# Attention tiles handled in pairs, and rotary tables loaded half a block earlier, in a transformer layer on 8 cores

## The reference

```
xn = layernorm(x)
x  = x + attn(xn) + ffn(xn)

# attn: 16 heads of 128, 4 key/value heads, causal
q, k = rope(rms_norm(xn @ Wq.T), rms_norm(xn @ Wk.T)); v = xn @ Wv.T
bias = einsum('bhsr,bhtr->bhst', Rq, Rk)        # 12 heads, rank 32, Rq = xn @ Wrq.T, Rk = xn @ Wrk.T
bias[:, :4] = (bias + bias.transpose(0,1,3,2)) * 0.5     # heads 0 to 3 are made symmetric
bias = bias * graph_scale;  heads 12 to 15 have no bias
out = softmax(mask(q k^T / sqrt(128) + bias)) v @ Wo.T

# ffn
gelu(xn @ W0.T + b0) @ W1.T + b1                # 2048 -> 8192 -> 2048
```

## Time and profile before

| | |
|---|---|
| time, median of 2 runs | 5299.11 us (5295.26 to 5302.97) |
| profiled execution | 5314.09 us |
| its span, first to last instruction of the slowest core | 5312.4 us |
| spans of all cores | 5275.7 to 5312.4 us |
| mean granted TensorE clock | 0.815 to 0.821 of full speed |
| TensorE matmuls | busy 3780.3 us, 71% |
| TensorE weight loads | busy 1343.7 us, 25% |
| ScalarE | busy 957.6 us, 18% |
| VectorE | busy 704.8 us, 13% |
| GpSimd | busy 458.6 us, 9% |
| the four query blocks | 659 to 3250 us of the span |
| feed-forward | 3260 to 5312 us of the span |

### The profile page before, as it was taken

The page is one execution under the profiler, slowest core; times in us unless marked ns, Lnnn a source line. Parts: engine busy times, 40 slices in busy tenths (PEclk is TensorE's granted clock), DMA queues, the critical chain, the costliest instruction groups (busy, mean ns, idle before and its releaser), DMA issues.

```text
span 5312.4 us, 42482 instructions; the slowest of 8 cores (5275.7 to 5312.4 us)
## 1 busy us (share of the span) xinstructions
PE 3780.3 (71%) x14112; PEld 1343.7 (25%) x14112; DVE 704.8 (13%) x1165; ACT 957.6 (18%) x1395; POOL 458.6 (9%) x548
## 2 busy tenths in 40 slices
PE   1367654446764775655775679988998899889987
PEld 0123111112111211112211123433333334333333
DVE  5522121112121111210101200000000000000000
ACT  1110022212232122232223351100110011001100
POOL 0000012211212011121011120000000000000000
PEclk9878566568576856767757789999999999999999
DMA  2201333243333433345223314445445544544454
GB/s 90 87 24 58 95 121 135 91 161 124 135 111 135 139 107 138 108 145 172 83 105 117 117 45 147 139 158 164 149 139 158 163 143 139 172 156 137 145 162 149
DMA packets 176454, 672.16 MB, mean 127 GB/s; under 512 B 22002, under 2 KB 30322, under 8 KB 152178
## 3 DMA queue, kind: packets, MB, share of 16 engines
q1 hardware_dynamic: 108146, 400.98, 23.7%
q10 hardware_dynamic: 36864, 159.40, 9.2%
q0 software_dynamic: 31232, 109.07, 5.1%
HBM read 560.32 MB, written 109.05 MB: 126 GB/s over the span
## 4 chain that ended last, share of the span: by engine, by line
PE 45%; DMA 34%; issue 5%; POOLq 5%; DVE 5%; ACT 4%; ACTq 1%; DVEq 1%; POOL 0%; SPq 0%
DMA wcbb<-wbf 18%; PE ps L723 14%; DMA wcbf<-w 9%; PE ps L750 8%; PE ps L488 5%; POOLq L131 5%; PE ps L295 3%; PE ps L619 3%; DMA wcbf<-wv 3%; PE ps L580 3%; PE ps L569 3%; DMA wbf<-wcbb 3%; PE ps L626 3%; PE ps L682 2%; ACT ar L600 1%
## 5 line engine op out<-in xcount | busy, mean ns | idle before, releaser
L750 PE MATMUL ps<-ar,wcbb 128*128 128x512 bf16 x4096 | 923.3, 382 | 155.0 <-DMA wcbb<-wbf 148.6
L723 PE MATMUL ps<-xnT,wcbb 128*128 128x512 bf16 x4096 | 914.3, 380 | 60.9 <-DMA wcbb<-wbf 44.0
L569 PE MATMUL ps<-ar 128*128 128x512 bf16 x640 | 336.4, 530 | 402.3 <-ACTq L131 400.4
L600 ACT ACTIVATE ar<-ps,cstS 128x512 bf16<-128x512 f32 x640 | 441.3, 690 | 980.1 <-DMA wcbf<-w 343.8
L750 PEld LDWEIGHTS ps<-ar,wcbb 128*128 128x128 bf16 x4096 | 388.6, 98 | 689.7 <-issue 263.7
L723 PEld LDWEIGHTS ps<-xnT,wcbb 128*128 128x128 bf16 x4096 | 386.7, 98 | 588.2 <-issue 161.2
L619 PE MATMUL ps<-ar 128*128 128x512 bf16 x640 | 332.6, 520 | 235.4 <-POOLq L131 235.2
L731 ACT ACTIVATE ar<-ps,b0S 128x512 bf16<-128x512 f32 x256 | 176.4, 689 | 1598.5 <-PE ps L723 1598.5
L488 PE MATMUL ps<-xnT,wcbb 128*128 128x512 bf16 x1024 | 273.1, 428 | 145.2 <-DMA wcbb<-wbf 85.5
L609 POOL TENSOR_TENSOR ar<-ar,maskS 128x512 bf16<-128x512 bf16 x256 | 294.5, 1150 | 795.8 <-ACTq L131 711.5
L682 PE MATMUL ps<-ar,wcbb 128*128 128x512 bf16 x1024 | 257.3, 411 | 128.6 <-DVEq L131 70.3
(11 more groups left out here) (70 smaller groups left out, 1521.4 us busy)
## 6 DMA issues: line engine op xcount, KB each, us to landing
wcbb<-wbf SPq DMA_DIRECT2D x608, 512.0 KB
wcbf<-w ACTq DMA_DIRECT2D x128, 1024.0 KB, 5.1
wbf<-wcbb POOLq DMA_DIRECT2D x160, 512.0 KB, 4.4
wcbf<-x SPq DMA_DIRECT2D x16, 1024.0 KB
wcbf<-wv SPq DMA_DIRECT2D x64, 256.0 KB
wcbf<-wq SPq DMA_DIRECT2D x16, 1024.0 KB
wcbf<-wo SPq DMA_DIRECT2D x16, 1024.0 KB
xtb<-xT ACTq DMA_DIRECT2D x64, 256.0 KB, 4.1
```

The costliest lines, as they stand in the source:

```text
L569: return e.matmul(bank[:, :], ar[:, KT_O + g * S + tt * 128: KT_O + g * S + (tt + 1) * 128], ar[:, QT_O + hh * 512:QT_O + hh * 512 + 512], ...
L600: e.activation(ar[:, PB_O + slot * 512:PB_O + (slot + 1) * 512], bank[:, :], AF.Exp, bias=cstS[:, C_NEGC:C_NEGC + 1])
L723: return e.matmul(bank[:, :], wcbb[:, slot * 2048 + ec * 128: slot * 2048 + (ec + 1) * 128], xnT[:, ec * S + sc * 512: ec * S + sc * 512 + ...
L750: return e.matmul(bank[:, :], wcbb[:, slot * 2048 + i * 128: slot * 2048 + (i + 1) * 128], ar[:, HACT_O + ncb * 512:HACT_O + (ncb + 1) * 512],
```

## The change

Three things change. The exponentials, masks and `av`/`den` matmuls of attention are handled in pairs of tiles: the exponentials of an even and the following odd tile run with one flush behind both, which frees both score banks; the masks of a pair follow with one flush behind both; and the order on TensorE becomes scores of tiles t - 1 and t, then `av` and `den` of the pair before. The making of the rotation tables becomes a function, `emit_qtables`, called once ahead of block 0 and then for the next block after Q of the second half has been rotated, ahead of the attention of that half; the sin piece has its own place in `fst`, so its load doesn't wait for VectorE's use of the cos piece. And in the rotations of K and Q `f_t2` writes into another buffer (`AM_RSBC`) than the one that `f_t1` reads, and the flush between the two is gone.

```diff
                 op("vector", f_t1)
-                flush("vector")
                 def f_t2(e, tcp=tcp):
-                    e.tensor_tensor(ar[:, AM_QRAW:AM_QRAW + 512], ps[3][:, :],
+                    e.tensor_tensor(ar[:, AM_RSBC:AM_RSBC + 512], ps[3][:, :],
...
-    for sc in range(NSC):
-        nt = 4 * (sc + 1)
-        v_c = dma("sync", fst[:, 0:512], d_cos[:, sc * 512:(sc + 1) * 512],
+
+    def emit_qtables(scn):
+        v_c = dma("sync", fst[:, 0:512], d_cos[:, scn * 512:(scn + 1) * 512],
                   (sDV, sDV.n))
+        v_s2 = dma("sync", fst[:, 512:1024], d_sin[:, scn * 512:(scn + 1) * 512],
+                   (sDV, sDV.n))
...
         op("vector", f_fqc, (sLD, v_c))
-        v_fq = flush("vector")
-        v_s2 = dma("sync", fst[:, 0:512], d_sin[:, sc * 512:(sc + 1) * 512],
-                   (sDV, v_fq))
...
         op("vector", f_fqs, (sLD, v_s2))
-        tab_dv = flush("vector")
-
+        v = flush("vector")
+        rs_free[0] = (sDV, v)
+        rs_free[1] = (sDV, v)
+        return v
+
+    tab_dv = emit_qtables(0)
+    for sc in range(NSC):
+        nt = 4 * (sc + 1)
...
             while rope_q:
                 rope_q.pop(0)()
+            if half == 1 and sc + 1 < NSC:
+                tab_dv = emit_qtables(sc + 1)
...
                     op("scalar", f_exp, (sPE, v_sc), pslot_free[slot])
+                    pend_t.append((tt, slot))
+                    if tt % 2 == 0:
+                        continue
                     v_exp = flush("scalar")
-                    sc_ps_free[par] = (sAC, v_exp)
-                    p_ready = (sAC, v_exp)
+                    sc_ps_free[0] = (sAC, v_exp)
+                    sc_ps_free[1] = (sAC, v_exp)
+                    p_pair = (sAC, v_exp)
                     if tt >= 4 * sc:
...
+                        for t2_, s2_ in pend_t:
+                            off = 128 * t2_ - 512 * sc
...
+                            op("gpsimd", f_msk, (sAC, v_exp))
+                        p_pair = (sGP, flush("gpsimd"))
...
+                    for t2_, s2_ in pend_t:
...
+                        av_q.append(mk_avden())
+                    pend_t = []
+                    while av_called[0] <= tt - 2:
+                        av_q[av_called[0]]()
+                        av_called[0] += 1
+                while av_called[0] < nt:
+                    av_q[av_called[0]]()
+                    av_called[0] += 1
```

More of the change, by code:

```diff
@@ L614, in build @@
-                    avb = ps[4 + (h % 2)]
[L615 to L625, removed]
-                                return e.matmul(ps[2][:, :], onesmS[:, :],
-                                                ar[:, PB_O + slot * 512:PB_O + (slot + 1) * 512],
-                                                start=(tt == 0), stop=(tt == nt - 1))
-                            v = pe(f_den, ps2_free if tt == 0 else (sPE, 0), inc=True)
-                            pslot_free[slot] = (sPE, v)
-                            dn["v"] = v
-                        return doit
@@ new lines, in build, with mk_avden, doit, f_av @@
+                        p_pair = (sGP, flush("gpsimd"))
+                    avb = ps[4 + (h % 2)]
+                    for t2_, s2_ in pend_t:
+                        def mk_avden(tt=t2_, slot=s2_, p_ready=p_pair, nt=nt,
+                                     avb=avb, g=g, h=h):
+                            def doit():
+                                def f_av(e, avb=avb, tt=tt, g=g, slot=slot, nt=nt):
+                                    return e.matmul(avb[:, :],
+                                                    ar[:, V_O + tt * 512 + g * 128:
+                                                       V_O + tt * 512 + (g + 1) * 128],
+                                                    ar[:, PB_O + slot * 512:PB_O + (slot + 1) * 512],
+                                                    start=(tt == 0), stop=(tt == nt - 1))
+                                pe(f_av, p_ready, av_free[h % 2] if tt == 0 else (sPE, 0))
+                                def f_den(e, tt=tt, slot=slot, nt=nt):
+                                    return e.matmul(ps[2][:, :], onesmS[:, :],
+                                                    ar[:, PB_O + slot * 512:PB_O + (slot + 1) * 512],
+                                                    start=(tt == 0), stop=(tt == nt - 1))
+                                v = pe(f_den, ps2_free if tt == 0 else (sPE, 0), inc=True)
+                                pslot_free[slot] = (sPE, v)
+                                dn["v"] = v
+                            return doit
+                        av_q.append(mk_avden())
```

25 lines of the change are left out of this document (9 added, 16 removed).

## The result

| | before | after |
|---|---|---|
| time, median of all runs (10 and 11) | 5312.67 us | 5350.35 us |
| profiled execution | 5314.09 us | 5347.98 us |
| its span, slowest core | 5312.4 us | 5346.3 us |
| spans of all cores | 5275.7 to 5312.4 us | 5305.7 to 5346.3 us |

The ratio after to before is 1.0078, 95% interval 1.0058 to 1.0097: slower by 0.8%, about 41 us, and less than the 2% that the chances went by. The mean of the eight cores' spans went from 5288.3 to 5321.7 us, +33.

The account below looks back on a forecast made before the run. Each attention head was taken as a serial chain: ScalarE's loads, tile loop, last masks, `f_rd1`, next loads. Attention +55 and tables -25.5 gave +29.5 us on 5299.1, so 5329 us (chance 0.50); range 5265 to 5375 us.

Parts of the forecast that it names:

- Part 1: Masks behind a spill write start only after its descriptor work: +3 us in block 0, +3 in block 1's heads 4 to 15.
- the other reading: Rival, chance 0.20: masks overlap the spill write's descriptor work, only the flush waits; -0.9 us a head, 5300 us.
- Part 2: Start of a head: tile 2's first matmul needs two exponentials and one flush, +0.7 us, down to +0.4 if they overlap.
- Part 3: Tile loop: +0 at the lower clock, +0.14 us a pair at the upper, +0.3 a pair without bias.
- Part 4: Ends of heads: +22 us in heads 0 to 3, +19 in heads 4 to 11, +7.5 in heads 12 to 15.
- The walk: Step-by-step timing of a head's end: last exponential to `f_rd1` 5.35 us in heads 0 to 3; +1.2 in heads 4 to 11.
- the clock is lost: Rival, chance 0.07: bubbles and mask waits keep heads 4 to 15 of blocks 2 and 3 at the lower clock; 5429 us.
- the cover: Block 2, heads 12 to 15: the third spill write still holds GpSimd when masks are due, hiding the added time: 0.
- Part 5: Tables moved from the block edges: TensorE's wait and slow first group go, about 8 to 9 us each edge, -25.5 us.
- Part 6: Rotary step: the flush taken from between `f_t1` and `f_t2` lies under the wait for the rotation matmul: 0.
- Only the tables: Rival, chance 0.10: transfers set the pace and cover the ends of heads, so only -25.5 us counts; 5273 us.
- The clock gained: Rival, chance 0.07: heads 0 to 3 of blocks 2 and 3 reach the upper clock for half their loop; 5265 us.

Follow-up runs that it names:

- e7: Kernel before with moved tables and rotary buffers; block 0 in pairs with all four masks under one flush, blocks 1 to 3 singly: 5302.37 us in one run.
- e6: Moved tables, full pairs in block 0; in blocks 1 to 3 paired exponentials and order, masks flushed one by one: ratio to before 1.0058.
- e9: As e4, but in blocks 1 to 3 TensorE's order goes by pairs, each exponential and mask keeping its own flush: ratio to before 0.9896.
- e10: As e9, but the masks of blocks 1 to 3 share a flush by pairs: 5278.35 us in the one run.
- e5: Moved tables, full pairs in block 0; in blocks 1 to 3 only masks share a flush, exponentials and order as before: ratio to before 1.0038.
- e1: Kernel before with only the table change and the rotary buffers, tiles handled singly in all blocks: ratio to before 0.9937.
- e3: Moved tables and rotary buffers, full pairs in block 0 only, blocks 1 to 3 handled singly: ratio to before 0.9902.
- e4: As e3, but in block 0 only the first two masks share a flush, the third and fourth have their own: ratio to before 0.9896.
- e8: As e4, plus the first two masks sharing a flush in block 1 heads 4 to 15 and block 2 heads 12 to 15: ratio to before 0.9895.

## Why the prediction was right, and where its steps were not

The forecast was 29.5 us more, 0.6%; measured were 0.8%, about 41 us, with the sign as forecast and the time inside the stated range. The sum of the loops came nearly as forecast too (57.2 against 55). But that nearness is in part luck, two errors that cancel: block 0 and block 1's last heads came 20 us better, and the late heads of blocks 1 to 3 worse by 23.

*Part 1, the spill write: wrong.* Of the two readings of the earlier trace rows I took the one by which descriptor work comes ahead of the masks, and forecast +3 for block 0. Measured -12.8: -1.1 us on average in the fourteen heads behind a write (median -1.0, from -0.5 to -2.1), near the other reading's -0.9, and +2.0 and +1.0 in heads 0 and 8, which have none. The step that failed is the inference "3.2 us less one mask is just the time at which the data was moving": the sum agreed, but a sum doesn't show an order. The row itself showed mask 0 from 0.62 us after the issue on, and I set that aside as a rough span. e7 shows that it was right. The earlier trace rows show when the data moved, and so can't tell whether the mask waited. The rule on DMAs issued from GpSimd (the Trainium skill, "DMA: Bandwidth & Descriptors", section "SWDGE vs HWDGE vs iDMA") may well be why the flush waits; no run here shows the descriptor work itself, and the masks don't wait for it.

*Part 2, the start: right.* 1924.36 to 1925.79 is 1.43 us, where before has 0.85: +0.58, inside the 0.4 to 0.7. Two exponentials take 1.27 and not 1.38; they overlap by 0.1.

*Part 3, the loop: right.* Two bias matmuls at the lower clock: 1939.87 to 1944.57 = 4.70 a pair, as before. At the upper clock 2.28 (2783.08 to 2785.36), the number forecast. Without bias a pair took 1.91, where 2.0 was forecast. The Trainium skill's page "Perfetto Trace Analysis", section "Matmuls", asks for groups that rotate through PSUM banks so that evacuation overlaps the next group. The runs agree with it: freeing both banks together costs 67 us of loops (e6 against e9). Little of that lies in the steady loop (15 us), and most at the starts and ends of heads (51).

*Part 4, the ends.* Heads 0 to 3 of blocks 1 to 3: forecast +1.85, measured +1.76, +1.75 and +1.74. The walk holds link by link: last exponential to `f_rd1` 1947.76 to 1953.03 = 5.27, forecast 5.35.

Heads 4 to 11 of blocks 2 and 3: mechanism right, size too small. Forecast +1.2, measured +1.73 and +2.13. First mask to `f_rd1`, 2792.22 to 2799.39, is 7.17 us, where the walk gave 6.1. A quarter of a microsecond is the mask pairs' distance, 2.75 and not 2.5. The rest is the clock: the walk let the last four matmuls run at the upper level, 1.1 us to `f_rd1`, and they took 1.96 (2797.43 to 2799.39), since the clock had fallen before them. Over all cores, a loop of these heads in block 3 had 10.8 us at the lower level before and has 13.9 after; of that, 0.6 us before and 3.3 after lie behind the clock's first rise in the loop. The clock falls more than half a microsecond ahead of `f_rd1` in 16 of the 64 heads before and in 58 after. So the rival "the clock is lost" was right in kind and wrong in its place. It isn't that these heads never rise; they rise and fall again in the last stretch, which costs the head above about a microsecond.

What makes it fall there is not shown. The waits for the mask pairs are at hand, but mask pairs alone don't do it: with the paired order and single exponentials (e10) the clock falls early in 17 of the 64, with mask pairs under the old order (e5) in 56, and with paired exponentials and single masks (e6) in 29. And in the head above the stretch at the upper level is as long as in the head of the earlier trace rows, 13.65 us (2781.80 to 2795.45 after, 2791.62 to 2805.27 before); before, the head was at its `f_rd1` 13.1 us behind the rise, after 17.6. So a head that takes longer from the rise to its end is a rival that no run tests.

Heads 12 to 15: forecast +1.9 in block 3 and 0 in block 2, measured +2.36 and +1.60. The step that failed for block 2 is the cover: the third write was to hide all of it. From the diagonal's third exponential to `f_rd1` such a head took 6.28 us before, and a head of block 3, with no write, 5.64, so the write can have held only some 0.6 us there. The pairs add 1.2 us ahead of that point (0.35 at the start, 0.8 in the pairs behind it), which no hold at the end could hide, and 0.4 behind it. The time at the lower clock grew as well, from 7.79 to 9.21 us a loop; whether as a cause or a consequence is open. Heads 4 to 11 of block 1: forecast +0.25, measured +0.65; heads 12 to 15 of it -0.7, where I forecast +0.25.

*Part 5, the tables.* Forecast -25.5, measured -21.2 (after) and -21.8 (e1). The last two edges gave 8.9 and 9.6, as forecast or a little more. The first gave 2.6, and the half's projection behind it came 2.0 us longer (1.3 in e1), so that edge is worth little. The 0.7 us ahead of block 0 did not show either (e1: +0.1). At the first edge the `wq` load needs the buffer that a write on GpSimd's queue still reads. After, the load follows the write's issue by 3.06 us (1229.94 to 1233.00). Before, the write was issued at 1249.32, and the same 3.06 behind it is 1252.4; the two tables held the load until 1254.21 (second row of the timeline of before), only 1.8 us longer. That the buffer is what the load waits for is read from the program and these times; no run moves the write. I had seen the late buffer and put it at the second group, with 1.7 us, where it is (1245.40 in the timeline after); but it is the first group's as well.

*Part 6, the rotary step*: 0 within what e1 can show, as forecast; no run has it alone.

*The rivals.* That the masks overlap the write was true as a mechanism; its 5300 us did not come, as the late heads lost more than forecast. Only the tables: fell, since the gaps between loops stayed at 430 us. The clock gained: fell, heads 0 to 3 of blocks 2 and 3 stay at 0.50 for 28.9 of 28.9 and 38.3 of 38.3 us of their loops.

**What stays open.** The times of e3, e4, e8 and e9 can't be told apart (0.9902, 0.9896, 0.9895, 0.9896), only their loops. Each is about 1% faster than before. Of those with the shorter block 0, e4 is the plainest: tables moved, pairs in block 0 alone, its masks flushed 2-1-1. Heads 12 to 15 of block 3 lose 0.76 us by the order alone (e9); 0.69 of it lies between the third exponential and the diagonal's first, and why is open.

## What to carry to other kernels

Before flushes are merged, ask for each what the later one hands on: here a flush freed a score bank that the next matmul needed, and sharing it cost 67 us of loops, while sharing one that stood behind a DMA issue and would have waited anyway was a gain. Where a wait is moved, read the waiting queue's order: the same mask flushes cost 62 us in the order that has scores queued behind the waiting matmul, and 13 in the order that has them ahead of it. And when two readings of one row differ only in the order of two things, no sum decides between them; take both into the range, or find the row whose start time does.

## What the runs showed of the hardware

A flush on GpSimd behind the issue of a 0.5 MB write ended 3.2 us after the issue, with one mask or two in between, and 5.4 us after it with four: the masks ran under the wait. TensorE's granted clock went from 1.00 to 0.50 inside one head's end, about half a microsecond after a wait of 1.38 us had ended and ahead of one of 1.11 us; in the head of the earlier trace rows, with single masks and waits of 0.80 us at most, it stayed at 1.00 to the head's end and fell 0.6 us behind it. Two masks in a row took 2.26 us, and the gap to the next pair in that head was 0.50.
